# Attention score tiles as a ring of three single PSUM banks, exponentials of 512 columns, four banks for the max pass

## The chip, the cores and the metric

The kernel runs on one core of one Trainium2 chip. The metric is device time in microseconds of one launch, median of the runs shown. All durations below come from one profiled execution of the kernel before.

## The reference

One transformer layer on x of shape (2, 2048, 256), in float32:

```
x = x + attention(layernorm(x))          # 16 heads of 16, scores * decay_mask before the softmax
x = x + ffn(layernorm(x))                # W1, W2 quantized to -1, 0, 1; relu between, 1024 wide

scores = q k^T / sqrt(16) * decay_mask   # decay_mask[h, q, k] = sum_n mix[h, n] * decay[h, n] ** |q - k|
probs  = softmax(scores);  out = probs v;  out Wo^T + bo
```

## The kernel before

Three stages follow each other: a token block (layer norm, q, k, v), the attention, and the feed-forward network. The change lies in the attention, which fills most of the span.

**Steps and slots.** The attention works in 16 steps (2 sequences by 8 pairs of heads), each of 32 *slots*. `for_steps` writes all 16 steps out one after the other, and every engine runs its own list of instructions. The order is fixed by hand in `step` of each engine; nothing reorders it but the semaphores. Four *units* of eight slots make a step: 2 heads by 2 halves of the queries. The softmax needs the row maximum first, so a max pass runs 12 slots (`LEAD`) ahead of the exponentials.

**One slot on PE** (`step` under `@block.tensor`) issues in this order: max pass items 0 and 1, score tile 2s, item 2, score tile 2s+1, item 3, then the products of the slot before (`products(s - 1)`). In one slot of each unit a transpose of the maxima (`turn_max`, L1506) is added.

- *Max pass* (`max_scores`, L1492): an item fills one 512-column bank of `ring`. DVE reduces it (L1272, L1274, L1276) and gives the bank back by `ring_free`. `ring` has three such banks and a fourth, `acc`, in which the products accumulate.
- *Score tile* (`scores`, L1523 and L1520): 128 keys by 1024 queries in two adjoining banks. There are two tiles, `tile0` and `tile1`, so four banks. A tile comes in two kinds, by `score_parts`: *plain* (two matmuls of 512 columns) or *diagonal* (512 columns in one bank; 256, 128 and a float32 transpose of 128, the raw block, in the other). A slot has two tiles of one kind, and half of the slots are of each kind. PE waits (`exp_done`) before tile t until the exponential of tile t-2 is done.
- *Exponential* (ACT, L1232): one instruction for the 1024 columns of a tile, from PSUM to `probs`. It waits for `tile_full`, which the last matmul of the tile raises.
- *Products* (`products`, L1539): four float32 matmuls of 512 columns, each 32 columns of the array wide, on the `probs` of the slot before.

**Also on ACT**, after the exponentials of some slots: a cast of 1024 columns for the next pair (`builder.cast`, L196, in slots 0, 1, 3, 4, 6, 8, 9, 11, 13 and 15 of a step), once per unit the copy of `acc` (`take_unit`, L1223, in slots 0, 8, 16 and 24, after `acc_full` by the last product of the unit), and once per unit a small copy (`repeat_max`, L1212). In slots 0 and 8 the copy of `acc` is followed by a cast.

**PSUM** has eight banks, all used: four for the tiles, three for `ring`, one for `acc`. The feed-forward network reuses them: `up` the four of the tiles, `attn` and `turn` the first two of `ring`, `down` the two behind them.

```
            pe.wait_ge(exp_done, EXPS * o + t + 1)      # scores(t): ACT raised it by 2 at the start
            ...
            act.wait_ge(tile_full, EXPS * o + t + 1)
            nc.scalar.activation(probs[:, t % 4], tile[t % 2][:]..., ACT.Exp, ...).then_inc(exp_done, 1)
```

Of the kernel before, what the change touches and what calls it, by code (L numbers as in the profile page):

```python
# [22 lines left out]
F32 = mybir.dt.float32  # L23
# [5 lines left out]
P = 128  # L29
# [656 lines left out]
UNIT_SLOTS = BLOCKS // 2  # L686
UNITS = 4
LEAD = UNIT_SLOTS + 4
RING = 3
ITEMS = 4  # L690
RED_SLOT, TURN_SLOT = 4, 5
RING_STEP = ITEMS * SLOTS + UNITS
AHEAD_ITEMS = ITEMS * LEAD + 1
EXPS = 2 * SLOTS
W_TURNS = 8
TOTAL_BANK = RING - 1
INVERT_SLOTS = (9, 10)
ATTN_SLOT, TOTAL_SLOT, ROOT_SLOT, Z_SLOT, SPLIT_SLOT = 22, 23, 24, 25, 26
W_SLOT = SLOTS - 5
# [38 lines left out]
def attention_and_ffn_block(nc, a, keep, builder, scr, out):  # L738
# [7 lines left out]
    with ExitStack() as ctx:  # L746
# [20 lines left out]
        cut = sb("cut", [P, 2])  # L767
        neg_cut = sb("neg_cut", [P, 2])
        heads_out = sb("heads_out", [P, 2, 512])
        tile = [ctx.enter_context(nc.psum_tensor(f"tile{t}", [P, 2, 512], F32)) for t in range(2)]  # L770
        ring = ctx.enter_context(nc.psum_tensor("ring", [P, RING + 1, 512], F32))
        acc = ring[:, RING]

# [28 lines left out]

        def up(f):

            return tile[f // 2 % 2][:, f % 2]


        tile_full = sem("tile_full")
# [34 lines left out]

        def turn_bank(q):

            return ring[:, (TOTAL_BANK + q) % RING]

        sums_loaded = [sem(f"sums_loaded{u}") for u in range(2)]
        x_loaded = [sem(f"x_loaded2_{u}") for u in range(2)]
# [317 lines left out]
        @block.scalar  # L1167
        def _(act):
            def cast(c, builds):
                if c == 0:  # L1170
                    act.wait_ge(qk_in, builder.loaded(builds))
                    for h in range(2):
                        act.wait_ge(raw_in[h], 2 * PART_DMAS * QUADS * builds)
                level, side = builder.at(c)
                if side == 0 and level in (0, 2):
                    for h in range(2):
                        for done in (q_in[h][0][level // 2], q_in[h][1][level // 2], k_in[h][level // 2]):
                            act.wait_ge(done, PART_DMAS * QUADS * builds)
                builder.cast(act, c, builds)

            def root(g):
                act.wait_ge(sqrt_in, g + 1)
                nc.scalar.activation(rstd[:], rstd[:], ACT.Sqrt).then_inc(sqrt_out, 1)

            def split_z(g):
                act.wait_ge(turned, g + 1)
                nc.scalar.copy(z_hi[:], turn[:]).then_inc(z_hi_ready, 1)  # L1187

            def split_heads(g):
                u = g % 2  # L1190
                act.wait_ge(heads_ready, g + 1)
                nc.scalar.copy(heads_hi[u], heads[u]).then_inc(heads_hi_ready, 1)

            def relu(g, f):
                bias = keep["b1_col"][:, f:f + 1]
                act.wait_ge(up_done, FC * g + f + 1)
                nc.scalar.activation(h_hi[:, f], up(f), ACT.Relu, bias=bias)  # L1197
                nc.scalar.activation(hidden[:, f], up(f), ACT.Relu, bias=bias).then_inc(up_taken, 1)  # L1198

            act.sem_inc(acc_free, 1)  # L1200
            for h in range(2):
                act.sem_inc(out_stored[h], QUADS)
            act.wait_ge(unit_ready, 1)
            for h in range(2):
                rows = k_stack[h][STACK:STACK + MAXROWS, 0:RAW].rearrange("p l x -> p (l x)")
                nc.scalar.copy(rows, unit[STACK:STACK + MAXROWS].broadcast_to([MAXROWS, RAW * SEQ])
                               ).then_inc(const_ready, 1)

            def repeat_max(par, count):

                act.wait_ge(max_ready, count)
                nc.scalar.copy(max_repeated[:], row_max[:, par].unsqueeze(1).broadcast_to([P, MAXROWS * RAW, UNIT_SLOTS])  # L1212
                               ).then_inc(repeated_ready, 1)


            nc.scalar.activation(warm[:], ident[:, 0:1], ACT.Exp)
            repeat_max(0, 1)
            act.sem_inc(exp_done, 2)
            def step(i, o, more):
                def take_unit(u):  # L1220
                    act.wait_ge(acc_full, UNITS * i + u + 1)
                    act.wait_ge(out_stored[u % 2], QUADS * (2 * i + u // 2 + 1))
                    nc.scalar.copy(heads_out[:, u % 2], acc[:]).then_inc(acc_free, 1)  # L1223

                for s in range(SLOTS):
                    act.wait_ge(probs_used, SLOTS * o + s + 1)
                    for t in (2 * s, 2 * s + 1):
                        u = s // UNIT_SLOTS + 1
                        if s % UNIT_SLOTS == TURN_SLOT and t % 2 and (more or u < UNITS):
                            repeat_max(u % 2, UNITS * i + u + 1)  # L1230
                        act.wait_ge(tile_full, EXPS * o + t + 1)
                        nc.scalar.activation(probs[:, t % 4], tile[t % 2][:].rearrange("p a b -> p (a b)"), ACT.Exp,  # L1232
                                             scale=1.0 / (SCALE * SCALE * HEAD_DIM ** 0.5)).then_inc(exp_done, 1)
                    if s % UNIT_SLOTS == 0 and (s > 0 or o > 0):
                        take_unit(s // UNIT_SLOTS - 1)
                    for c in range(CHUNKS):
                        if more and hi_slot[c] == s:
                            cast(c, i + 1)
                    if not more and s == ROOT_SLOT:
                        root(0)  # L1240
                    if not more and s == SPLIT_SLOT:
                        split_z(0)
                if o == STEPS - 1:
                    take_unit(UNITS - 1)

            for_steps(step)
            for g in range(GROUPS):
                for f in range(FC):
                    relu(g, f)
                    if f == 3 and g + 1 < GROUPS:  # L1250
                        root(g + 1)
                    if f == 4 and g + 2 < GROUPS:
                        split_heads(g + 2)
                if g + 1 < GROUPS:
                    split_z(g + 1)

        @block.vector
        def _(dve):
# [41 lines left out]
            def invert(g):  # L1300
                u = g % 2
                dve.wait_ge(p_sums_loaded[u], 2 * QUADS * (g // 2 + 1))
                if g >= 2:
                    dve.wait_ge(inv_stored[u], QUADS * (g // 2))
                nc.vector.tensor_tensor(p_sums[:], p_sums_in[:, u, 0], p_sums_in[:, u, 1], ALU.add).then_inc(p_sums_added, 1)
                dve.wait_ge(p_sums_added, g + 1)
                nc.vector.reciprocal(inv[:, u], p_sums[:]).then_inc(inv_ready, 1)
# [164 lines left out]
        def _(pe):  # L1472
# [36 lines left out]
            def scores(t, o):  # L1509

                u, kb = t // BLOCKS, t % BLOCKS
                h, half = u // 2, u % 2
                pe.wait_ge(exp_done, EXPS * o + t + 1)
                started = set()
                for level, first, width in score_parts(kb, half):
                    col = first - half * HALF
                    bank, at = col // 512, col % 512
                    out = tile[t % 2][:, bank, at:at + width]
                    if level == RAW:
                        last = nc.tensor.matmul(out, diag[h][:, kb], ident[:], is_transpose=True,  # L1520
                                                start=bank not in started, stop=True, skip_group_check=True)
                    else:
                        last = nc.tensor.matmul(out, k_stack[h][:, level, kb * P:(kb + 1) * P],  # L1523
                                                q_stack[h][:, half, level, col:col + width],
                                                start=bank not in started, stop=True, skip_group_check=True)
                    started.add(bank)
                last.then_inc(tile_full, 1)

            def products(j, o):

# [2 lines left out]
                h = u // 2  # L1533
                for par in range(2):
                    t = 2 * j + par
                    pe.wait_ge(exp_done, EXPS * o + t + 3)
                    for qt in range(2):
                        row = (2 * par + qt) * ROWS
                        last = nc.tensor.matmul(acc[row:row + ROWS], v_ones[h][:, t % BLOCKS],  # L1539
                                                probs[:, t % 4, qt * 512:(qt + 1) * 512],  # L1540
# [29 lines left out]
            def up_product(g, f):  # L1570
                if f == 0:
                    pe.wait_ge(z_hi_ready, g + 1)
                if g == 0 and f == 0:
                    pe.wait_ge(w_taken, W_TURNS // 2)
                if FC * g + f >= 4:
                    pe.wait_ge(up_taken, FC * g + f - 3)
                for part in (z_hi, z_lo):
# [7 lines left out]
            def down_bias(g):  # L1585
                if g == 0:
                    pe.wait_ge(b2_ready, 1)
                    pe.wait_ge(w_taken, W_TURNS)
                    pe.wait_ge(acc_free, UNITS * STEPS + 1)
                else:  # L1590
                    pe.wait_ge(result_ready, g)
                for t in range(TILES):
# [17 lines left out]
            def turn_w(q):  # L1610
# [2 lines left out]
                pe.wait_ge(ternary_ready, m + 1)  # L1613
                if q == 1:
                    pe.wait_ge(z_lo_ready, 1)
                if q >= RING:
                    pe.wait_ge(w_taken, q - RING + 1)
                for j in range(4):
                    if m == 0:
                        src = rows[:, (q % 2) * 4 + j, (q // 2) * P:(q // 2 + 1) * P]  # L1620
# [121 lines left out]
```

## Time and profile before

| | |
|---|---|
| runs | 1788.88, 1789.5, 1789.95 us (median 1789.5) |
| profiled execution, first to last instruction | 1787.4 us |
| PE busy | 1744.3 us, 98% |
| DVE busy | 1558.8 us, 87% |
| ACT busy | 1345.2 us, 75% |
| POOL busy | 776.5 us, 43% |

The profiled execution is known by its span of 1787.4 us; the median of the runs is 2.1 us above it. PE is TensorE (matmuls), PEld its weight loads, DVE VectorE, ACT ScalarE, POOL GpSimd. The records of matmuls overlap, since a matmul is still draining while the next streams: a busy share of PE says that something was in flight, and the time from the start of one matmul to the start of the next says how fast they go through. The chain of waits gives the pieces by that second measure.

### The profile page before, as it was taken

To read this page: it belongs to the slowest core of one execution; us is meant where nothing else is said; L and a number is where in the kernel's file an instruction comes from. 1 tells how busy PE (TensorE), PEld (TensorE's weight loads), DVE (VectorE), ACT (ScalarE), POOL (GpSimd) and SP (SyncE) were. 2 spreads that over 40 slices of the span, in tenths; PEclk is the share of its full clock that TensorE was granted. 3 is DMA by queue.
4 is the path that set the end of the run, shared out by engine and by line. 5 is a ranking of instruction groups with operands and counts; after the bars stand their busy time and mean duration, and the time that the engine had idled before them with its cause. 6 is when DMAs were issued, how large, how long until landed. Compare 5 with 4: busy or idle time off the path is not lost.

```text
span 1787.4 us, 31962 instructions
## 1 busy us (share of the span) xinstructions
PE 1744.3 (98%) x11858; PEld 775.6 (43%) x11858; DVE 1558.8 (87%) x3664; ACT 1345.2 (75%) x1558; POOL 776.5 (43%) x405
## 2 busy tenths in 40 slices
PE   7979999999999999999999999999999999998998
PEld 4524444444444444444444444444444444444666
DVE  5879988999899989898999999898989999987885
ACT  5748687878787777878787878687878787667565
POOL 4009182726354554637271809181727364150110
PEclk9959999999999999999999999999999999999999
DMA  6884747474655546464637373747474645444541
GB/s 199 274 211 106 157 97 162 97 157 101 134 118 120 134 107 139 99 153 104 149 90 156 83 155 86 153 95 161 97 162 97 142 108 112 115 123 110 136 120 36
DMA packets 177835, 230.33 MB, mean 129 GB/s; under 512 B 92640, under 2 KB 113520, under 8 KB 167536
## 3 DMA queue, kind: packets, MB, share of 16 engines
q1 hardware_dynamic: 175744, 227.61, 54.6%
q8 instruction: 94, 1.54, 0.4%
q0 software_dynamic: 80, 0.54, 0.2%
q14 instruction: 61, 0.50, 0.1%
q10 hardware_dynamic: 1856, 0.14, 0.1%
HBM read 65.94 MB, written 36.45 MB: 57 GB/s over the span
## 4 chain that ended last, share of the span: by engine, by line
PE 87%; DVE 5%; ACT 1%; issue 1%; ACTq 0%; DVEq 0%
PE ring L1539 28%; PE ring L1492 27%; PE tile L1523 23%; PE tile L1520 3%; PE tile L1581 2%; PE ring L1600 2%; DVE part_max L1272 1%; PE ring L1506 1%; DVE qk L1362 1%; DVE z_lo L1358 1%; DVE stats L1334 1%; DVE decayed L1330 0%; ACT z_hi L1187 0%; PE ring L1567 0%; DVE lo L1314 0%
## 5 line engine op out<-in xcount | busy, mean ns | idle before, releaser
L1232 ACT ACTIVATE probs<-tile 128x1024 f32<-128x1024 f32 x1024 | 1000.3, 1023 | 331.4 <-PE tile L1520 183.8
L1272 DVE TENSOR_REDUCE part_max<-ring 128x1 f32<-128x512 f32 x1536 | 964.9, 683 | 122.1 <-PE ring L1492 120.1
L1492 PE MATMUL ring<-k_stack,q_stack 96*128 96x512 f16 (+2 forms) x3072 | 714.5, 314 | 11.2 <-SPq L211 9.7
L1523 PE MATMUL tile<-q_stack,k_stack 98*128 98x512 f16 (+2 forms) x2560 | 585.0, 326 | 0.3
L1539 PE MATMUL ring<-probs,v_ones 128*32 128x512 f32 x4096 | 546.8, 605 | 0.0
L1492 PEld LDWEIGHTS ring<-k_stack,q_stack 96*128 96x128 f16 x3072 | 263.9, 99 | 511.5 <-DVE part_max L1272 393.2
L1101 POOL TENSOR_TENSOR diag<-diag,row_max 128x1024 f32<-128x1024 f32 x64 | 121.6, 1900 | 629.9 <-DVE row_max L1285 629.9
L1523 PEld LDWEIGHTS tile<-q_stack,k_stack 98*128 98x128 f16 x2560 | 249.6, 98 | 275.0 <-ACT probs L1232 5.9
L188 POOL TENSOR_TENSOR decayed<-qk,table_in 128x1024 f32<-128x1024 f32 x120 | 282.9, 2363 | 8.0
L1274 DVE TENSOR_REDUCE part_max<-ring 128x1 f32<-128x384 f32 x512 | 279.6, 546 | 0.7 <-PE ring L1492 0.7
L202 POOL TENSOR_TENSOR lo<-decayed,hi 128x1024 f16<-128x1024 f32 x120 | 256.7, 2139 | 9.9 <-ACT hi L196 9.9
L1276 DVE CUSTOM_DVE_ANT_0 diag<-ring,mask 128x128 f32<-128x128 f32 x512 | 143.5, 280 | 2.0
L202 POOL TENSOR_TENSOR lo<-qk,hi 128x1024 f16<-128x1024 f32 x30 | 64.1, 2136 | 183.7 <-ACT hi L196 183.7
L1520 PE MATMUL tile<-ident,diag 128*128 128x128 f32 x512 | 143.1, 280 | 0.0
L196 ACT CAST hi<-decayed 128x1024 f16<-128x1024 f32 x128 | 133.8, 1045 | 6.8 <-POOL decayed L188 3.0
L1539 PEld LDWEIGHTS ring<-probs,v_ones 128*32 128x32 f32 x4096 | 81.0, 108 | 56.9 <-issue 3.0
L1520 PEld LDWEIGHTS tile<-ident,diag 128*128 128x128 f32 x512 | 71.6, 140 | 6.8
L1197 ACT ACTIVATE diag<-tile,b_col 128x512 f16<-128x512 f32 x64 | 44.0, 688 | 40.0 <-PE tile L1581 40.0
L1362 DVE TENSOR_TENSOR qk<-probs,diag 128x512 f16<-128x512 f32 x64 | 45.0, 703 | 27.7 <-ACT probs L1198 27.7
L1106 POOL TENSOR_TENSOR diag<-diag,bo_all 128x1024 f32<-128x1024 f32 x8 | 18.8, 2354 | 108.6 <-DMA diag<-in_x 108.6
L1198 ACT ACTIVATE probs<-tile,b_col 128x512 f32<-128x512 f32 x64 | 43.9, 686 | 0.0
L1600 PE MATMUL ring<-hi,diag 128*128 128x256 f16 x256 | 38.5, 273 | 5.1 <-DVE qk L1362 5.0
(154 smaller groups left out, 967.8 us busy)
## 6 DMA issues: line engine op xcount, KB each, us to landing
q_stack<-hi SPq DMA_DIRECT2D x320, 128.0 KB, 3.8
k_stack<-hi SPq DMA_DIRECT2D x128, 256.0 KB, 4.3
q_stack<-lo SPq DMA_DIRECT2D x160, 128.0 KB, 3.1
table_in<-table_scratch SPq DMA_DIRECT2D x64, 256.0 KB, 8.1
k_stack<-lo SPq DMA_DIRECT2D x64, 256.0 KB, 3.7
out_scratch<-heads_out SPq DMA_DIRECT2D x64, 256.0 KB, 3.3
k_stack<-hi SPq DMA_DIRECT2D x64, 128.0 KB, 3.4
lo<-out_scratch SPq DMA_DIRECT2D x32, 256.0 KB, 5.3
```

Of the source, the lines that this page charges most:

```text
L188: ops.tensor_tensor(self.source(c), self.half_view(self.qk[:], level, side), self.factors(level, side), ALU.mult).then_inc(self.decayed_re ...
L196: self.nc.scalar.copy(self.half_view(self.hi[:, level], level, side), self.source(c)).then_inc(self.hi_ready, 1)
L202: ops.tensor_tensor(self.half_view(self.lo[:, level], level, side), self.source(c), self.half_view(self.hi[:, level], level, side), ALU.su ...
L1101: nc.gpsimd.tensor_tensor(part, part, row_max[:, half].unsqueeze(2).broadcast_to([P, UNIT_SLOTS, P]), ALU.subtract).then_inc(diag_ready, 1)
L1232: nc.scalar.activation(probs[:, t % 4], tile[t % 2][:].rearrange("p a b -> p (a b)"), ACT.Exp, scale=1.0 / (SCALE * SCALE * HEAD_DIM ** 0. ...
L1272: nc.vector.tensor_reduce(out[:, k:k + 1], ring_bank(n), AX.X, ALU.max).then_inc(ring_free, 1)
L1274: nc.vector.tensor_reduce(out[:, 3:4], ring_bank(n)[:, 0:3 * P], AX.X, ALU.max).then_inc(blocks_seen, 1)
L1276: nc.vector.tensor_tensor_reduce(out=diag[h][:, q], in0=ring_bank(n)[:, 3 * P:4 * P], in1=mask[h][:], scale=1.0, scalar=-3.0e38, op0=ALU.m ...
L1492: last = nc.tensor.matmul(ring[:, n % RING, col:col + width], q_stack[h][0:STACK, q // UNIT_SLOTS, level, q0:q0 + P], k_stack[h][0:STACK, ...
L1520: last = nc.tensor.matmul(out, diag[h][:, kb], ident[:], is_transpose=True, start=bank not in started, stop=True, skip_group_check=True)
L1523: last = nc.tensor.matmul(out, k_stack[h][:, level, kb * P:(kb + 1) * P], q_stack[h][:, half, level, col:col + width], start=bank not in s ...
L1539: last = nc.tensor.matmul(acc[row:row + ROWS], v_ones[h][:, t % BLOCKS], probs[:, t % 4, qt * 512:(qt + 1) * 512], start=(j % UNIT_SLOTS = ...
```

## The change

The two double banks become one tensor `tile` of three single banks, and the bank that this frees goes to `ring`, now four banks for the max pass and `acc` behind them. A bank n = 4s .. 4s+3 of a slot holds half a tile. PE waits before bank n until the exponential of bank n-3 is done, and raises `tile_full` per bank. ACT issues four exponentials of 512 columns per slot in place of two of 1024, each on one bank. The products wait per bank. The order of the work on PE stays but for the diagonal tiles, whose parts are now issued bank by bank. The feed-forward network takes `acc` as its fourth `up` bank; a wait on DVE is added in `invert`; the turned weights keep their three banks.

```diff
-RING = 3
+RING = 4
+TILE_BANKS = 3
+W_BANKS = 3
...
-EXPS = 2 * SLOTS
+EXPS = 4 * SLOTS
...
-        tile = [ctx.enter_context(nc.psum_tensor(f"tile{t}", [P, 2, 512], F32)) for t in range(2)]
+        tile = ctx.enter_context(nc.psum_tensor("tile", [P, TILE_BANKS, 512], F32))
...
-            return tile[f // 2 % 2][:, f % 2]
+            return acc if f % 4 == TILE_BANKS else tile[:, f % 4]
...
-            act.sem_inc(exp_done, 2)
+            act.sem_inc(exp_done, TILE_BANKS)
...
-                    for t in (2 * s, 2 * s + 1):
+                    for n in range(4 * s, 4 * s + 4):
                         u = s // UNIT_SLOTS + 1
-                        if s % UNIT_SLOTS == TURN_SLOT and t % 2 and (more or u < UNITS):
+                        t, half = n // 2, n % 2
+                        if s % UNIT_SLOTS == TURN_SLOT and n % 4 == 2 and (more or u < UNITS):
                             repeat_max(u % 2, UNITS * i + u + 1)
-                        act.wait_ge(tile_full, EXPS * o + t + 1)
-                        nc.scalar.activation(probs[:, t % 4], tile[t % 2][:].rearrange("p a b -> p (a b)"), ACT.Exp,
+                        act.wait_ge(tile_full, EXPS * o + n + 1)
+                        nc.scalar.activation(probs[:, t % 4, half * 512:(half + 1) * 512],
+                                             tile[:, (EXPS * o + n) % TILE_BANKS], ACT.Exp,
...
@@ invert @@
+                if g >= 1:
+                    dve.wait_ge(inv_ready, g)
...
-                pe.wait_ge(exp_done, EXPS * o + t + 1)
-                started = set()
-                for level, first, width in score_parts(kb, half):
...
-                last.then_inc(tile_full, 1)
+                for x in range(2):
+                    n = EXPS * o + 2 * t + x
+                    pe.wait_ge(exp_done, n + 1)
+                    parts = [p for p in score_parts(kb, half) if (p[1] - half * HALF) // 512 == x]
...
+                        out = tile[:, n % TILE_BANKS, at:at + width]
...
+                    last.then_inc(tile_full, 1)
...
-                    pe.wait_ge(exp_done, EXPS * o + t + 3)
                     for qt in range(2):
+                        pe.wait_ge(exp_done, EXPS * o + 2 * t + qt + 1 + TILE_BANKS)
...
+                if g == 0 and f == TILE_BANKS:
+                    pe.wait_ge(acc_free, UNITS * STEPS + 1)
```

**Where instructions move.** On PE, one plain slot in the middle of a unit. `tile` is the score banks, `ring<-k_stack` the max pass, `ring<-probs` the products. Before:

```order
L1492 MATMUL ring<-k_stack,q_stack 128x512 [waits ring_free] x2
L1523 MATMUL tile<-q_stack,k_stack 128x512 [waits exp_done]
L1523 MATMUL tile<-q_stack,k_stack 128x512
L1492 MATMUL ring<-k_stack,q_stack 128x512 [waits ring_free]
L1523 MATMUL tile<-q_stack,k_stack 128x512 [waits exp_done]
L1523 MATMUL tile<-q_stack,k_stack 128x512
L1492 MATMUL ring<-k_stack,q_stack 128x256 [waits ring_free]
L1492 MATMUL ring<-k_stack,q_stack 128x128 x2
L1539 MATMUL ring<-probs,v_ones 32x512 [waits exp_done]
L1539 MATMUL ring<-probs,v_ones 32x512
```

and the same slot now:

```order
L1498 MATMUL ring<-k_stack,q_stack 128x512 [waits ring_free] x2
L1530 MATMUL tile<-q_stack,k_stack 128x512 [waits exp_done] x2
L1498 MATMUL ring<-k_stack,q_stack 128x512 [waits ring_free]
L1530 MATMUL tile<-q_stack,k_stack 128x512 [waits exp_done] x2
L1498 MATMUL ring<-k_stack,q_stack 128x256 [waits ring_free]
L1498 MATMUL ring<-k_stack,q_stack 128x128 x2
L1545 MATMUL ring<-probs,v_ones 32x512 [waits exp_done] x4
```

No matmul was added or taken away and none of these changed place; each 512-column score matmul and each product now has a wait of its own. On ACT, a slot with a cast behind it, before:

```order
L1232 ACTIVATE probs<-tile 128x1024 [waits tile_full,probs_used]
L1232 ACTIVATE probs<-tile 128x1024 [waits tile_full]
L196 CAST hi<-decayed 128x1024 [waits decayed_ready]
```

and now:

```order
L1235 ACTIVATE probs<-tile 128x512 [waits tile_full,probs_used]
L1235 ACTIVATE probs<-tile 128x512 [waits tile_full] x3
L196 CAST hi<-decayed 128x1024 [waits decayed_ready]
```

The cast stays behind the last exponential of its slot.

## Rows read from the trace of the kernel before

**Rows 1.** The page: an engine's busy time, and PE's granted clock in 40 slices.

```profile
PE 1744.3 (98%) x11858; PEld 775.6 (43%) x11858; DVE 1558.8 (87%) x3664; ACT 1345.2 (75%) x1558; POOL 776.5 (43%) x405
...
PEclk9959999999999999999999999999999999999999
```

**Rows 2.** Windows over one diagonal and one plain slot: length, busy time, clock, DMA.

```profile
702.50:705.47 2.97, 2.97 (x23) 1.37 (x22) 2.55 (x7) 2.18 (x3) 2.83 (x3) 1.00 1.04 221
705.47:708.31 2.84, 2.84 (x19) 1.05 (x18) 2.66 (x8) 2.84 (x4) 2.84 (x2) 1.00 0.08 24
```

**Rows 3.** Chain of waits, core stretch, two slots: start us, us, what.

```profile
701.96 0.54 PE ring L1492 x2
702.50 0.38 PE tile L1523 x3
702.88 0.12 PE tile L1520
...
703.93 1.00 PE ring L1539 x8
704.93 0.54 PE ring L1492 x2
705.47 0.43 PE tile L1523 x2
705.90 0.22 PE ring L1492
...
706.78 1.00 PE ring L1539 x8
```

**Rows 4.** Groups by line and form: busy us, mean ns | idle before, releaser.

```profile
L1232 ACT ACTIVATE probs<-tile 128x1024 f32<-128x1024 f32 x1024 | 1000.3, 1023 | 331.4 <-PE tile L1520 183.8 <-PE tile L1523 144.3
L1523 PE MATMUL tile<-q_stack,k_stack 98*128 98x512 f16 x1536 | 500.3, 380 | 0.3
...
L1198 ACT ACTIVATE probs<-tile,b_col 128x512 f32<-128x512 f32 x64 | 43.9, 686 | 0.0
...
L1223 ACT COPY heads_out<-ring 128x512 f32<-128x512 f32 x64 | 37.5, 586 | 1.2 <-PE ring L1539 1.2
...
L1187 ACT CAST z_hi<-ring 128x1024 f16<-128x1024 f32 x8 | 8.1, 1013 | 3.4 <-PE ring L1567 3.4
```

**Rows 5.** Timeline at 702 us, exponential after an idle ACT, products: start, us, what.

```profile
702.72 0.28 PE L1520 MATMUL tile<-ident,diag 128*128 128x128 f32 x1
...
703.09 1.94 ACT L1232 ACTIVATE probs<-tile 128x1024 f32<-128x1024 f32 x2 [0.85 <-PE tile L1520]
...
703.86 0.16 PEld L1539 LDWEIGHTS ring<-probs,v_ones 128*32 128x32 f32 x8
```

**Rows 6.** Chain of waits, last step, where PE waited for an exponential.

```profile
1595.62 1.95 ACT probs L1232 x2
1597.57 0.05 issue
1597.62 0.60 PE tile L1523 x2
```

**Rows 7.** Line 1492 at 704 us: ns min/median/max; the 390 is behind the products.

```profile
L1492 PE MATMUL ring<-k_stack,q_stack x3: 379/379/390, 704.9 to 705.7; 96*128 96x512 f16 x3
```

**Rows 8.** Timeline at 344 us: a new slot, and ACT with copy and cast.

```profile
344.60 0.11 PEld L1492 LDWEIGHTS ring<-k_stack,q_stack 96*128 96x128 f16 x2 [0.84 <-DVE part_max L1272]
...
344.76 0.59 ACT L1223 COPY heads_out<-ring 128x512 f32<-128x512 f32 x1
...
345.25 1.05 ACT L196 CAST hi<-decayed 128x1024 f16<-128x1024 f32 x1
...
346.19 1.03 ACT L1232 ACTIVATE probs<-tile 128x1024 f32<-128x1024 f32 x1
```

**Rows 9.** Windows: the max pass alone (98 to 128), and slots without it.

```profile
98.00:128.00 30.00, 26.74 (x68) 6.76 (x68) 27.93 (x71) 15.66 (x5) 1.89 (x1) 0.50 0.82 177
1598.00:1602.30 4.30, 4.30 (x33) 1.60 (x32) 2.05 (x3) 3.61 (x5) 4.16 (x3) 1.00 0.04 9
```

**Rows 10.** Waits over the whole span: total us, times, longest.

```profile
PEld ring L1492 <- DVE part_max L1272: 393.2, 502, 1.0
```

**Rows 11.** Timeline of the last step, a weight load behind products.

```profile
1599.15 0.11 PEld L1506 LDWEIGHTS ring<-ident,max_repeated 128*64 128x64 f32 x1 [0.84 <-issue]
```

More of the change, by code:

```diff
@@ L693 @@
 AHEAD_ITEMS = ITEMS * LEAD + 1
-EXPS = 2 * SLOTS
+EXPS = 4 * SLOTS
 W_TURNS = 8
-TOTAL_BANK = RING - 1
+TOTAL_BANK = W_BANKS - 1
 INVERT_SLOTS = (9, 10)
@@ L844, in turn_bank @@
         def turn_bank(q):
-            return ring[:, (TOTAL_BANK + q) % RING]
+            return ring[:, (TOTAL_BANK + q) % W_BANKS]
         sums_loaded = [sem(f"sums_loaded{u}") for u in range(2)]
@@ L1512, in scores @@
                 h, half = u // 2, u % 2
-                pe.wait_ge(exp_done, EXPS * o + t + 1)
-                started = set()
-                for level, first, width in score_parts(kb, half):
[L1516 to L1526, printed above, removed]
-                last.then_inc(tile_full, 1)
+                for x in range(2):
+                    n = EXPS * o + 2 * t + x
+                    pe.wait_ge(exp_done, n + 1)
+                    parts = [p for p in score_parts(kb, half) if (p[1] - half * HALF) // 512 == x]
+                    for j, (level, first, width) in enumerate(parts):
+                        at = first - half * HALF - x * 512
+                        out = tile[:, n % TILE_BANKS, at:at + width]
+                        if level == RAW:
+                            last = nc.tensor.matmul(out, diag[h][:, kb], ident[:], is_transpose=True,
+                                                    start=(j == 0), stop=True, skip_group_check=True)
+                        else:
+                            last = nc.tensor.matmul(out, k_stack[h][:, level, kb * P:(kb + 1) * P],
+                                                    q_stack[h][:, half, level, first - half * HALF:first - half * HALF + width],
+                                                    start=(j == 0), stop=True, skip_group_check=True)
+                    last.then_inc(tile_full, 1)
             def products(j, o):
@@ L1588, in down_bias @@
                     pe.wait_ge(w_taken, W_TURNS)
-                    pe.wait_ge(acc_free, UNITS * STEPS + 1)
                 else:
@@ L1615, in turn_w @@
                     pe.wait_ge(z_lo_ready, 1)
-                if q >= RING:
-                    pe.wait_ge(w_taken, q - RING + 1)
+                if q >= W_BANKS:
+                    pe.wait_ge(w_taken, q - W_BANKS + 1)
                 for j in range(4):
```

## The prediction

> **What bounds the kernel now.** I read the page first: PE is busy 98% of the span at the full granted clock but for the ends [rows 1]. A busy PE need not be PE at its peak, so the next view is the chain of waits in a stretch of the core. All of its pieces are PE's [rows 3], and the window over each slot agrees: PE busy 2.97 of 2.97 us in a diagonal slot and 2.84 of 2.84 in a plain one, at clock 1.00 [rows 2]. The same pieces come back in every slot. A score matmul of 512 columns takes 0.22 us from start to start, which is what it has to stream, a score tile 0.43 or 0.50, the products 1.00. PE waits for nobody here. DVE works 2.55 and 2.66 us of such a slot [rows 2], so it is some 0.3 us from the bound and follows PE. ACT waits 331 us in all for PE before its exponentials [rows 4]. The path is PE's list of instructions, 512 slots long.
>
> **What the change adds and removes.** On PE not one matmul is added, removed or made shorter. Since no slot holds a wait of PE's that could go, a gain has no place to come from; the question is what waits come in.
>
> *Fourth bank for the max pass.* It lets PE write an item while DVE is one more reduction behind. The wait table puts 393 us of PEld's idle time on these reductions [rows 10], which looks like the prize. But the wait ends when the products have streamed: the same 0.84 us of idle PEld stands before a weight load in the last step that follows products and whose releaser is "issue", not DVE [rows 11]. I cost the fourth bank at 0. Its cover is the 1.00 us of products, which hides the reductions. DVE can't gain on PE either, since the order on PE is fixed.
>
> *Bank ring of three, plain slot.* Before, tile t waited for the exponential of t-2, issued a whole slot earlier. Now bank n waits for that of bank n-3. For the last bank of a slot (n3) that is the exponential of the first (n0) **of the same slot**. Banks n0, n1 and n2 wait for exponentials of the slot before, which had the 1.00 us of products to finish.
> - Time that PE has between the starts of n0 and n3, from the chain: n0 and n1 0.43, item 2 0.22, n2 0.22, together 0.87 [rows 3], 0.86 less rounded.
> - Time that the loop needs: the matmul of n0, 0.38 from start to its modelled end [rows 4]; to the exponential, 0.10 more (the transpose that starts at 702.72 and takes 0.28 is followed by an exponential at 703.09) [rows 5]; the exponential, D; from its end to PE's next start, 0.05 [rows 6]; 0.01 for a matmul whose weights weren't loaded ahead (390 ns against 379) [rows 7].
> - D isn't in the trace for 512 columns. From PSUM, 1024 columns took 1013 ns as a cast and 512 columns 586 as a copy, so 512 columns are worth 427. The exponential of 1024 took 1023; less 427 that is **0.596** [rows 4], spaced 0.49 apart, since the long ones are spaced 0.92 (two in 1.94, one of them 1.02) [rows 5]. Lower bound 0.51, half of 1023 with no fixed part; upper bound 0.69, the relu of 512 columns that reads a bias [rows 4]. I take 0.596, next to the copy's 0.586, whose form is nearest.
> - Loop 0.38 + 0.10 + 0.596 + 0.05 + 0.01 = 1.14, less 0.86 = **0.28 us** of idle PE per plain slot.
>
> *Diagonal slot.* The bank with the raw block takes 0.38 + 0.12 - 0.22 = 0.28 [rows 3]. With the raw block in n0: its transpose starts 0.16 in and ends 0.28 later, so the loop is 0.16 + 0.28 + 0.10 + 0.596 + 0.05 + 0.01 = 1.20 against 0.28 + 0.22 + 0.22 + 0.28 = 1.00. With it in n1: 1.14 against 0.93. Both give **0.20 to 0.21**.
>
> Nothing hides these stalls: item 3, the products and the next slot are queued behind n3 on PE. Items 2 and n2 already stand between and are counted.
>
> *Where ACT comes late to n0.* After slots 0 and 8 of a step ACT copies `acc` and then casts. The copy can't start before the unit's last product is done: it starts 0.16 us into the next slot, the next exponential 1.59 in [rows 8]. In the kernel before that delay is absorbed, the next need being a slot away. Now n0's exponential would start at 0.44 + 0.48 = 0.92 (plain) or 0.98 (raw) into the slot, so n3 comes 0.6 later still. Two slots in each of 15 steps: 30 x 0.61 = **18 us**. A cast alone does no harm: the four exponentials begin at 0.92 and the last ends at some 2.98 of a 3.1 us slot; with 0.94 of cast behind it ACT is free at about 3.8, before 3.1 + 0.92. Nor does `repeat_max` (0.13).
>
> *ACT's sum.* Four spaced 0.49 make 1.97 us per slot instead of 1.84, +66 us in all, beside PE. With casts and copies (0.37 per slot) ACT has 2.34 of 3.1: not the bound.
>
> *The rest at nothing:* the waits of the products per bank (exponentials of the slot before, long done; today all eight of their weight loads pass in 0.16 us, across the wait that stands in their middle [rows 5]), the order within diagonal tiles (as many matmuls), `invert`, the fourth `up` bank (`acc` is free before the network begins). Longer slots give POOL and the loads more time; they were not waited for.
>
> **Sum.** In 500 slots with the max pass, 248 plain x 0.28 = 69 us and 252 diagonal x 0.202 = 51. Late copies 18. The last 12 slots have no items 2 between, but there PE already waits for exponentials [rows 6], so the loop of three banks adds only about 0.2 us to the slots that wait for nothing else, 2 us. Together **140 us**. Against the profiled span, 1787 + 140 = 1927; the median of the runs stood 2.1 above that span, so 1789.5 + 140 = **1929.5 us**.
>
> **Rivals.**
> 1. *D is long* (0.69, as the relu). The loop grows by 0.09: 500 x 0.09 = 45, and with some casts now late to n0, about 50 more: **1980 us**. For it: an exponential may fetch a bias as the relu does. Against: at 1024 columns it costs 10 ns more than a plain cast. 11%.
> 2. *D is short* (0.51): 500 x 0.085 = 43 less, **1887 us**. That there is a fixed part is seen in the copy (586, not 507) [rows 4]. 5%.
> 3. *PE's clock falls.* In the max pass alone, where PE waits for DVE between its matmuls, the granted clock is 0.50, 1.2 GHz; in slots of the last step where PE stood idle for exponentials it stayed at 1.00, 2.4 GHz [rows 9]. If the new idle in every slot let it fall in a tenth of the slots, each would cost another 2.84 less 0.28: 51 x 2.56 = 131 us, **2060 us**. 3%. The Trainium skill, TensorE: Matmul & The Clock Gate, section on a second failure mode (psum-queue depth-cycling), says that short idles of PE as it goes through PSUM banks make the clock alternate between its two levels; by that rule this rival is the rule and not the exception. The trace so far does not bear it out: the last step had longer idles at 1.00.
> 4. *The fourth bank pays* (the side below). If the wait table is right in that PE's weight loads are held by DVE, the loads may start one reduction earlier, 0.60 of the 0.84 us: 512 x 0.60 = 307 gained, 140 lost, **1622 us**. It decides from 0.27 us per slot on. For it: [rows 10]. Against: PE is streaming products in that time, and [rows 11]. 3%, and 1% that it just balances.
>
> **How the numbers follow.** The forecast has 77%: 1905 (late copies cost nothing and the tail too) to 1955 (D 0.62 and copies later). The range takes in rivals 1 and 2 at their ends, **1887 to 1980**, and leaves out 3 and 4 and what is beyond. A measurement of this kernel can tell about 0.2% from no change. Faster by more: 0.03; within: 0.01; slower: 0.96.
>
> **What would show it.** In the profile after: a group of ACT exponentials 128x512 x2048 of about 596 ns; a wait of PEld's score load for the exponential in nearly every slot, some 0.2 to 0.5 us of idle load each; slots of 3.11 to 3.12 (plain) and 3.17 (diagonal), 3.7 behind the copy with cast, at clock 1.00; the chain alternating between PE and ACT; DVE's wait for `ring` up by as much as PE's stall; no change in the wait of the max items. The prediction is wrong if slots stay at 2.84, if D is outside 0.51 to 0.69, if the last bank of a slot isn't the one that waits, or if ACT has no idle time left.

## The result and the profile after

The changed kernel takes **1928.85 us** (median of 4 runs, 1928.51 to 1930.11) against 1789.72 (4 runs, 1788.88 to 1789.96): a ratio of 1.0784, 95% interval 1.077 to 1.0797, so 139 us slower. The profiled execution spans 1926.7 us, 139.3 more than before.

The page of the changed kernel, engines and PE's granted clock, where [rows 1] stood before:

```profile
span 1926.7 us, 32986 instructions
...
PE 1828.8 (95%) x11858; PEld 753.1 (39%) x11858; DVE 1581.8 (82%) x3664; ACT 1414.8 (73%) x2582; POOL 777.8 (40%) x405
...
PEclk9969999999999999999999999999999999999999
```

PE went from 98% to 95%. The granted clock stayed at full, 1.00 over the whole stretch from 135 to 1750 us. A page hardly shows a loss of 7.8%: 139 us of span came, of which 84.5 count as busy PE, because the records of matmuls cover most of each short wait. The groups by line, where [rows 4] stood:

```profile
L1235 ACT ACTIVATE probs<-tile 128x512 f32<-128x512 f32 x2048 | 1065.2, 602 | 387.3 <-PE tile L1530 284.4 <-PE tile L1527 94.4
...
L1530 PE MATMUL tile<-q_stack,k_stack 98*128 98x512 f16 x1536 | 545.0, 382 | 54.4 <-ACT probs L1235 28.8
...
L1530 PEld LDWEIGHTS tile<-q_stack,k_stack 98*128 98x128 f16 x2560 | 239.9, 98 | 473.6 <-ACT probs L1235 276.5 <-issue 0.8
```

and the last of these before:

```profile
L1523 PEld LDWEIGHTS tile<-q_stack,k_stack 98*128 98x128 f16 x2560 | 249.6, 98 | 275.0 <-ACT probs L1232 5.9 <-issue 1.5
```

The exponential of 512 columns took 602 ns (0.596 forecast). The score matmul is as long as before (382 against 380 ns), so no work got slower. What is new is idle time before PE's score weight loads, 473.6 us in place of 275.0, and the exponentials as its releaser. The waits of the whole span:

```profile
PEld ring L1498 <- DVE part_max L1280: 320.0, 385, 0.8
ACT probs L1235 <- PE tile L1530: 284.4, 292, 3.0
PEld tile L1530 <- ACT probs L1235: 276.5, 515, 3.9
...
DVE part_max L1276 <- PE ring L1498: 198.0, 374, 0.6
...
PEld ring L1498 <- DVE part_max L1276: 65.8, 96, 0.8
```

The third row is the stall: before, this wait came 9 times in the whole program and held 5.9 us; now it comes 515 times in 512 slots and holds 276.5 us of idle PEld. Loads stood idle for 275.0 us before too, with PE busy 98% of the span, so this is more than PE lost: about half of it, 139 us, is time added. The first and last row together are the wait that the fourth bank was to relieve: 385.8 us in 481 times, where [rows 10] had 393.2 in 502. It is still there, with another reduction's name on it. DVE's own wait for PE (the fourth row; `L1276` is the reduction that was `L1272`) went from 120.1 to 198.0 us: DVE was slowed by PE, not PE by DVE.

The chain of waits over one plain slot, start us, us, what, where [rows 3] stood:

```profile
809.62 0.54 PE ring L1498 x2
810.15 0.23 PE tile L1530
810.39 0.02 issue
810.41 0.02 ACTq L1234
810.42 0.04 issue
810.47 0.61 ACT probs L1235
811.08 0.05 issue
811.12 0.39 PE tile L1530
811.51 0.22 PE ring L1498 x3
811.74 0.99 PE ring L1545 x8
```

From 809.62 to 812.73 the slot takes 3.11 us (2.84 before). The path leaves PE behind n0 (the 0.23) and runs through 0.08 of issue and queue, 0.61 of exponential, 0.05 of issue, and back to n3 (the 0.39). Bank n1, item 2 and n2 don't appear: they are done inside that loop. What follows n3 has its old lengths. In a diagonal slot the stall shows less, since the long bank gives PE more to do:

```profile
803.26 0.54 PE ring L1498 x2
803.80 0.38 PE tile L1530 x3
804.18 0.12 PE tile L1527
804.30 0.22 PE ring L1498
804.52 0.22 PE tile L1530
804.74 0.03 issue
804.76 0.34 PE tile L1530 x2
805.10 0.12 PE tile L1527
805.22 0.22 PE ring L1498 x3
805.44 0.99 PE ring L1545 x8
806.44 0.54 PE ring L1498 x2
```

3.18 us from 803.26 to 806.44, against 2.97. Here the view keeps to PE and shows the loop only as 0.03 of issue ahead of n3. The rest is in the next row: 0.34 for the first two matmuls of n3, which took 0.17 where they followed others at once (as the same pair does in [rows 3], 0.38 less the 0.22 of the long one). The view counts n2 to its modelled end, and n3, started afresh behind it, is counted from start to modelled end too, which is 0.17 longer. 0.03 + 0.17 = 0.20. A gap on PE has to be measured from slot to slot, not read off an "issue" row.

The slot behind a copy and a cast, on the timeline (start, us, engine):

```profile
540.73 2.07 ACT L1235 ACTIVATE probs<-tile 128x512 f32<-128x512 f32 x4 [1.18 <-PE tile L1527]
...
543.08 0.59 ACT L1225 COPY heads_out<-ring 128x512 f32<-128x512 f32 x1 [0.29 <-PE ring L1545]
...
543.57 1.05 ACT L196 CAST hi<-qk 128x1024 f16<-128x1024 f32 x1
...
544.51 2.06 ACT L1235 ACTIVATE probs<-tile 128x512 f32<-128x512 f32 x4
...
545.16 0.10 PEld L1530 LDWEIGHTS tile<-q_stack,k_stack 98*128 98x128 f16 x1 [0.82 <-ACT probs L1235]
```

The copy starts when the last product of the unit is done, the cast follows, n0's exponential begins 1.58 us into the slot, which starts at 542.93 (0.15 before the copy, as in [rows 8]), and n3 waits for it to 545.17. This slot takes 3.785 us. The trace has 29 such slots, all of this length.

### The profile page after: what moved, and what is told of

Same layout as the page of the kernel before. It is cut to its first block, busy times and chain, and to the rows that moved or that the text cites. A ratio compares the mean times of both kernels' runs of the same rounds, so it can differ in the third digit from the quotient of the medians.

```text
span 1926.7 us, 32986 instructions
## 1 busy us (share of the span) xinstructions
PE 1828.8 (95%) x11858; PEld 753.1 (39%) x11858; DVE 1581.8 (82%) x3664; ACT 1414.8 (73%) x2582; POOL 777.8 (40%) x405
## 4 chain that ended last, share of the span: by engine, by line
PE 76%; ACT 11%; issue 4%; DVE 4%; ACTq 0%; DVEq 0%
PE ring L1545 27%; PE ring L1498 21%; PE tile L1530 20%; ACT probs L1235 9%; PE tile L1527 3%; PE ring L1607 2%; PE tile L1589 1%; DVE part_max L1276 1%; PE ring L1512 1%; DVE qk L1368 1%; ACT heads_out L1225 1%; DVE z_lo L1364 0%; PE ring L1589 0%; DVE stats L1340 0%; PE ring L1573 0%
## 5 line engine op out<-in xcount | busy, mean ns | idle before, releaser
L1235 ACT ACTIVATE probs<-tile 128x512 f32<-128x512 f32 x2048 | 1065.2, 602 | 387.3 <-PE tile L1530 284.4
L1276 DVE TENSOR_REDUCE part_max<-ring 128x1 f32<-128x512 f32 x1536 | 965.7, 684 | 202.9 <-PE ring L1498 198.0
L1530 PE MATMUL tile<-q_stack,k_stack 98*128 98x512 f16 (+2 forms) x2560 | 687.7, 328 | 59.8 <-ACT probs L1235 30.2
L1530 PEld LDWEIGHTS tile<-q_stack,k_stack 98*128 98x128 f16 x2560 | 239.9, 98 | 473.6 <-ACT probs L1235 276.5
L1278 DVE TENSOR_REDUCE part_max<-ring 128x1 f32<-128x384 f32 x512 | 283.5, 554 | 18.3 <-PE ring L1498 18.2
L1199 ACT ACTIVATE diag<-tile,b_col 128x512 f16<-128x512 f32 x48 | 33.1, 689 | 33.3 <-PE tile L1589 33.3
L1225 ACT COPY heads_out<-ring 128x512 f32<-128x512 f32 x64 | 37.5, 586 | 19.0 <-PE ring L1545 19.0
```

What stands on the lines that cost most here:

```text
L1235: nc.scalar.activation(probs[:, t % 4, half * 512:(half + 1) * 512], tile[:, (EXPS * o + n) % TILE_BANKS], ACT.Exp, scale=1.0 / (SCALE * S ...
L1276: nc.vector.tensor_reduce(out[:, k:k + 1], ring_bank(n), AX.X, ALU.max).then_inc(ring_free, 1)
L1278: nc.vector.tensor_reduce(out[:, 3:4], ring_bank(n)[:, 0:3 * P], AX.X, ALU.max).then_inc(blocks_seen, 1)
```

## Experiments

Slots below are from the starts of the products' matmuls in each trace, medians over the steps, given as plain / diagonal. The kernel before: 2.841 / 2.971; the changed one: 3.113 / 3.178.

### The score ring back to four banks

```diff
-RING = 4
-TILE_BANKS = 3
+RING = 3
+TILE_BANKS = 4
```

(and the wait for `acc_free` back in `down_bias`)

> Score ring of four single banks, max pass back on three, exponentials still 512 wide: only the depth of the score ring is undone. Theory (the stall is the wait of bank n3 for the exponential of n0 in the same slot): bank n now waits for that of n-4, a whole slot back, so PE's slots return to 2.84 and 2.97 us and the time to 1790 us (1788 to 1793), although ACT has 66 us more of exponentials than before. Rival (narrower exponentials are the cost, ACT has become the bound): the time stays near 1929, at least 1855 (1790 + 66).

Measured: 1788.88 us against 1788.16 for the kernel before on the same chip, ratio 1.0003 (0.9993 to 1.0012); slots 2.841 / 2.974. Exponentials of this kernel and a piece of its chain:

```profile
L1235 ACT ACTIVATE probs<-tile 128x512 f32<-128x512 f32 x2048 | 1064.0, 606 | 257.9 <-PE tile L1530 184.5 <-PE tile L1527 72.4
```

```profile
904.15 0.54 PE ring L1498 x2
904.69 0.43 PE tile L1530 x2
905.12 0.22 PE ring L1498
905.34 0.43 PE tile L1530 x2
905.77 0.22 PE ring L1498 x3
906.00 0.99 PE ring L1545 x8
```

The halved exponentials cost 64 us of ACT and nothing of the time. All of the 139 us come from the depth of the ring; the rival, ACT as the bound, is out.

### The max pass back to three banks, the rest as changed

```diff
+MAX_BANKS = 3
...
-                    if n + AHEAD_ITEMS - RING + 1 > 0:
-                        pe.wait_ge(ring_free, RING_STEP * o + n + AHEAD_ITEMS - RING + 1)
+                    if n + AHEAD_ITEMS - MAX_BANKS + 1 > 0:
+                        pe.wait_ge(ring_free, RING_STEP * o + n + AHEAD_ITEMS - MAX_BANKS + 1)
...
-                        last = nc.tensor.matmul(ring[:, n % RING, col:col + width],
+                        last = nc.tensor.matmul(ring[:, n % MAX_BANKS, col:col + width],
```

(and the same in `turn_max` and in DVE's `ring_bank`)

> The change with its max pass on three banks, the fourth left idle: only the gift to the max pass is taken back. Theory (the fourth bank is worth nothing, PE's idle weight loads before the max items are the products streaming): 1929 us, within 2 us. Rival (the fourth bank pays part of the loss back): slower than 1929 by what it pays, up to 307 us if 0.60 us per slot, 47 us if only the 0.09 us between the two spacings behind a group of products (545 against 453 ns).

Measured: 1928.99 us, ratio to before 1.0783 (1.0767 to 1.0799); slots 3.113 / 3.178. The fourth bank brought nothing that can be measured.

### Item 3 ahead of bank n3

```diff
-                    scores(2 * s + 1, o)
+                    scores(2 * s + 1, o, (0,))
+                    late = s % BLOCKS == BLOCKS - 1
+                    if late:
+                        scores(2 * s + 1, o, (1,))
+                    if ahead:
+                        max_scores(s, s + LEAD, (3,), i, o)
+                    if not late:
+                        scores(2 * s + 1, o, (1,))
...
-                    if ahead:
-                        max_scores(s, s + LEAD, (3,), i, o)
```

In slots 15 and 31 the old order has to stay, since item 3 releases the stack that n3 still reads.

> The change with item 3 of the max pass issued before score bank n3 in place of behind it, in 30 of 32 slots. Theory: 0.22 us more work lies between n0 and n3, so the plain slots' stall of 0.28 shrinks to about 0.06 and the diagonal one's 0.21 to 0: slots of 2.89 to 2.91 and 2.97, 1827 us (1820 to 1835). Rival (PE waits for something that doesn't depend on what stands between n0 and n3, such as the extra waits themselves): 1929.

Measured: 1828.6 us in one run (before 1789.34); slots 2.890 / 2.975, 3.177 in slots 15 and 31, which kept the old order, and 3.56 behind copy and cast. 100 us are won back by moving item 3 past one bank. PE had as many waits as before, so it is not the waits that cost but what stands inside the loop.

### No cast behind the copy

```diff
-        hi_slot = (0, 1, 3, 4, 6, 8, 9, 11, 13, 15)
+        hi_slot = (1, 2, 3, 4, 6, 7, 9, 11, 13, 15)
```

> The change with no cast behind the copy of acc: the casts of slots 0 and 8 go elsewhere (slots 1, 2, 3, 4, 6, 7, 9, 11, 13, 15). Theory: 30 slots lose 0.6 to 0.67 us each, 19 us, so 1910 us, and no slot of 3.78 is left. Rival (those slots are long because the copy alone is late, or because POOL's chain behind the casts is late): under 5 us change, or slower.

Measured: **1966.25 us**, slower than the change by 37 us (ratio to before 1.0989, 1.0972 to 1.1005). The theory held for the slots behind the copies, which fell to 3.18 and 3.11. The total went the way of the rival, a slower kernel through POOL's chain: slot 4 grew to 5.5 us or more in all 15 steps that have casts, and slot 5 to 4.2 to 4.6 in 12 of them. ACT's timeline at one slot 4:

```profile
771.82 1.10 ACT L1235 ACTIVATE probs<-tile 128x512 f32<-128x512 f32 x2
773.02 4.65 POOL L188 TENSOR_TENSOR decayed<-qk,table_in 128x1024 f32<-128x1024 f32 x2
775.47 1.04 ACT L196 CAST hi<-decayed 128x1024 f16<-128x1024 f32 x1 [2.55 <-POOL decayed L188]
776.42 2.05 ACT L1235 ACTIVATE probs<-tile 128x512 f32<-128x512 f32 x4
777.06 0.10 PEld L1530 LDWEIGHTS tile<-q_stack,k_stack 98*128 98x128 f16 x1 [2.98 <-ACT probs L1235]
```

The third cast waits 2.55 us for a product of POOL. POOL makes that product only behind the rest of the second cast, and I had moved the second cast one slot later and left the third where it was. All exponentials queue behind the waiting cast, and PE's n3 behind them (2.98 us of idle PEld, 2.48 of idle PE).

That explains slot 4 and not slot 5. The windows (length, busy time, clock, DMA) of slots 4 and 5 of this step, and of slot 5 of another step:

```profile
772.11:777.61 5.50, 3.02 (x21) 1.00 (x19) 2.76 (x7) 2.95 (x6) 5.36 (x3) 1.00 0.21 55
777.61:782.10 4.49, 4.49 (x21) 1.20 (x19) 2.72 (x7) 2.99 (x7) 4.49 (x4) 0.62 0.01 4
...
568.22:571.34 3.12, 3.02 (x21) 0.97 (x19) 2.56 (x7) 2.99 (x7) 3.12 (x3) 1.00 0.00 0
```

In the long slot 5 PE is busy all the time, and its granted clock is lower. Within it, from 777.80 to 781.20 us, it is 0.50 (1.2 GHz). In each of the 15 steps PE stood idle for 2.48 us in slot 4. In 12 of them the clock fell to 0.50 behind that; in three it stayed at 1.00 and slot 5 took 3.11 (there slot 8 took 3.5). The page has a 9 in each of its clock slices there and does not show this.

I went on from the cause in slot 4 and shifted the first casts together:

```diff
-        hi_slot = (0, 1, 3, 4, 6, 8, 9, 11, 13, 15)
+        hi_slot = (1, 2, 4, 5, 7, 9, 10, 12, 14, 15)
```

> The change with the casts in slots 1, 2, 4, 5, 7, 9, 10, 12, 14 and 15: no cast behind the copy of acc, and the distances between the first casts as in the kernel before, so that POOL's products are there when ACT comes to them. In the run with the casts of slots 0 and 8 moved, slots 1 and 9 fell to 3.18 and 3.11 as the theory has it, but slots 4 and 5 grew to 5.5 and 4.4, with a cast that waited 2.55 us for POOL. Theory: 30 slots lose 0.6 to 0.67 us and none gains, 1910 us (1907 to 1914). Rival (moving casts always starts POOL's chain late): still above 1929.

Measured: 1910.28 us (ratio to before 1.0685, 1.0667 to 1.0703), no slot of 3.78 left. The late copies cost 18.6 us, as one run less the other gives (1928.85 - 1910.28; the kernel before took 1789.7 and 1788.8 us beside them, so this is good to about 1 us). Against this run, the core of the one with the unlucky casts is 56.3 us longer: 36.8 in slot 4 and 15.8 in slot 5. The wait in slot 4 is 15 x (5.50 - 3.18) = 35 us of that; some 18 us, by estimate, are what the lower clock cost, namely what is left of these two slots.

### A longer exponential

```diff
-                                             tile[:, (EXPS * o + n) % TILE_BANKS], ACT.Exp,
+                                             tile[:, (EXPS * o + n) % TILE_BANKS], ACT.Exp, bias=no_bias[:],
```

> The change with exponentials that read a bias of zeros from a tile of its own, a way to make D longer. Theory: each ns of D is a ns of every one of 500 slots, 0.5 us per ns. If D goes from 602 to the relu's 687 ns, 1973 us (slots of 3.20 and 3.27); if the bias costs nothing, D and the time stay. Rival (the wait isn't the loop through ACT's latency): time unchanged with D longer.

Measured: 1979.76 us in one run; slots 3.203 / 3.267, and more in the slots behind a cast.

```profile
L1236 ACT ACTIVATE probs<-tile,no_bias 128x512 f32<-128x512 f32 x2048 | 1249.7, 693 | 282.4 <-PE tile L1532 212.3 <-PE tile L1529 69.6
```

(`no_bias` is a tile of one column of zeros.) D rose by 91 ns (693 against 602) and the slots by 90 and 89. That gives 45 us over 500 slots; the other 6 of the 51 are slots in which ACT, now with less slack, came to n0 late (3.26 behind casts). An exponential with a bias from a tile behaves as the relu did.

### A ring of two banks

```diff
+SCORE_BANKS = 2
...
-            act.sem_inc(exp_done, TILE_BANKS)
+            act.sem_inc(exp_done, SCORE_BANKS)
```

(and `% SCORE_BANKS` for the banks of scores and exponentials, `+ SCORE_BANKS` in the products' wait)

> The change with a score ring of two banks, one step further. Theory: n2 waits for n0's exponential and n3 for n1's, of the same slot. Loop 1.15 against 0.65 between them: 0.50 us more per slot, slots of 3.61 and 3.67, 2180 us (2160 to 2200), clock still 1.00 in the core. Rival (the clock rule: many short idles of PE make the granted clock alternate): the granted clock under 1.00 in part of the core, and over 2250 us.

Measured: 2177.93 us in one run; slots 3.600 / 3.667. The granted clock in 40 slices, and the window over the core (the 1.00 is the clock):

```profile
PEclk9879999999999999999999999999999999999999
```

```profile
135.00:1990.00 1855.00, 1642.07 (x10118) 576.03 (x10118) 1377.26 (x3199) 1273.12 (x2286) 740.60 (x354) 1.00 0.44 98
```

With some 0.76 us of idle array in each plain slot, 21% of it, the clock stayed at full (2.4 GHz) through the core. That bears on the rule cited as a rival, from the Trainium skill, TensorE: Matmul & The Clock Gate, on psum-queue depth-cycling: this kernel cycles through PSUM banks with a short idle of PE in every slot, and with those idles no alternation is seen in the core of this run or of the changed kernel. The clock did go back and forth in the core of the run with the casts moved, and in the one below that has this placing too, each time behind an idle of PE of 2.4 to 2.7 us, which is not one of the short ones of the ring.

### Score banks and max items alternating

```diff
-                        max_scores(s, s + LEAD, (0, 1), i, o)
+                        max_scores(s, s + LEAD, (0,), i, o)
...
-                    scores(2 * s, o)
+                    scores(2 * s, o, (0,))
+                    if ahead:
+                        max_scores(s, s + LEAD, (1,), i, o)
+                    scores(2 * s, o, (1,))
                     if ahead:
                         max_scores(s, s + LEAD, (2,), i, o)
-                    scores(2 * s + 1, o)
+                    scores(2 * s + 1, o, (0,))
...
```

(item 3 and n3 as in the run above, swapped in slots 15 and 31)

> The change with max items and score banks alternating on PE and nothing moved on ACT. Theory: no stall but in the 30 slots behind copy and cast, which keep some 0.6 to 0.7 us: slots 2.85 and 2.98 (as in the run with both edits, in all slots but 4 and 5), 1812 us (1806 to 1818). Rival (the 1870 us of the run with both edits came from the alternation): near 1870.

Measured: 1814.45 us (ratio 1.0147, 1.0132 to 1.0162); slots 2.850 / 2.978, with 3.56 left behind copy and cast. The order alone gives back 114 of the 139 us.

With both edits, first with the unlucky placing of the casts:

> The change with max items and score banks alternating (item 0, n0, item 1, n1, item 2, n2, item 3, n3; the last two swapped in slots 15 and 31) and no cast behind the copy of acc (casts in slots 1, 2, 3, 4, 6, 7, 9, 11, 13, 15). Theory: 1.3 us lie between n0 and n3 against a loop of 1.15, so no stall is left and three banks do what four did: slots 2.84 and 2.97, 1792 us (1789 to 1797). The fourth bank of the max pass brings nothing below that. Rival (waits per bank keep weight loads from being pulled ahead, or the alternation costs): above 1805.

Measured: 1869.97 us (ratio 1.0452, 1.0434 to 1.047). Missed, and for what was found above: slot 4 took 5.5 to 5.9 us in all 15 steps through a cast that waited for POOL, and behind it the granted clock fell to 0.50 in 11 of them (slot 5 at 4.5 to 5.4, slot 6 at up to 4.7). In the other four slot 8 took 4.3, its cast waiting 1.4 us for POOL. The other slots were at 2.85 / 2.98. Then with the casts shifted together:

> Both: alternating order on PE and the casts in slots 1, 2, 4, 5, 7, 9, 10, 12, 14 and 15. Theory: no stall of the score ring is left; 1794 us (1790 to 1798), some 0.01 us per slot above the kernel before, as in the slots of the run with both edits (2.85 and 2.98 against 2.84 and 2.97). It doesn't beat the kernel before, since PE's stream of matmuls is the same and the fourth bank of the max pass hides nothing that wasn't hidden. Rival (with DVE fed more evenly and a fourth bank, DVE's slack turns into a gain): under 1786.

Measured: **1802.92 us** (ratio 1.0081, 1.0066 to 1.0096), 9 us over what I expected. The slots are right but for two in each step: slot 16 takes 3.34 and slot 11 3.05. The timeline at slot 16:

```profile
838.74 1.04 ACT L196 CAST hi<-decayed 128x1024 f16<-128x1024 f32 x1 [0.63 <-POOL decayed L188]
...
839.69 2.05 ACT L1235 ACTIVATE probs<-tile 128x512 f32<-128x512 f32 x4
...
840.34 0.10 PEld L1530 LDWEIGHTS tile<-q_stack,k_stack 98*128 98x128 f16 x1 [0.36 <-ACT probs L1235]
```

The last cast, moved next to the one before it, waits 0.63 us for POOL; the cast ahead of slot 11 waits 0.17. These two slots are 0.36 + 0.20 us a step, 8.4 us in 15 steps. I did not try a further placing, as even without them (1794.5) the kernel would not beat the one before.

## Why the prediction was right

It said 1929.5 us, and 1928.85 was measured. The mechanism is the one that was forecast, and the terms hold one by one to within 4 us. That the sum came out within 1 us is luck: the plain slots were put 4 us too high, and the other three terms together about 3 us too low.

- **PE's list is the path and no slot has slack.** Right. Where the stall is taken away (four banks), the slots return to their old lengths to within 0.003 us, with 64 us more work on ACT.
- **D = 0.596 us**: 0.602. The longer exponential showed the slope: 90 ns of slot for 91 ns of D.
- **Plain slot +0.28, diagonal +0.20 to 0.21**: 3.113 - 2.841 = 0.272 and 3.178 - 2.971 = 0.207. The 31 plain slots that hold the transpose of the maxima lose only 0.20 (3.24 against 3.04), for a cause that I did not look for. So the plain slots cost 217 x 0.272 + 31 x 0.20 = 65 us, where I had 69, and the diagonal ones 252 x 0.207 = 52, where I had 51. The chain shows the loop in its parts: 0.08 where I took 0.10, 0.61 with the part to the exponential's end, 0.05 back.
- **Copy and cast, 18 us**: 18.6, by taking them away. There were 29 such slots, not 30 (slot 0 of the first step has no copy behind it). The added length is 3.785 less 3.113 or 3.178, 0.64 on average, against 0.61: I took the diagonal slot's value for all, and half of them are plain, at 0.67.
- **Fourth bank 0**: 0 within the intervals, in a run of its own. The row by which I judged it (the same idle time before a weight load that no reduction holds [rows 11]) was the right one; the wait table's releaser was not.
- **The last 12 slots, 2 us**: in the trace of the changed kernel this stretch is 2.8 us longer than before. The run with four banks has it 2.6 us shorter, so it varies by as much as the term, and the term is not settled.
- Rival 1 is what the run with the bias became: 1979.8 for 1980. Rival 3 did not happen, even with almost three times the idle time per slot. But the ground on which I set it aside was misread: in the window of the last step in [rows 9] PE is busy 4.30 of 4.30 us, so it shows no idle of PE at the full clock. The trace before has such a window later, at 1609 to 1614 us: PE busy 1.82 of 5.00 us at 1.00. And the mechanism is real here: behind the longer idles of the moved casts the clock fell to 0.50. Which idles are too long, these runs do not show. Rival 4 is out by the run with three banks. Rival 2 never applied: ACT's fixed part per instruction is there.

Two of the signs were off. I looked for a chain alternating between PE and ACT: it does so in plain slots, but in diagonal ones it stays on PE. And DVE's wait was to grow by as much as PE's stall, but its row grew by 78 us of the 139. "A cast alone does no harm" holds only for a cast whose input is there, which the moved casts taught me, and only with this D: with the longer exponential the slots behind a cast took 3.26 in place of 3.20.

## What to carry to other kernels

Count a ring's depth in the consumer's round trip: find the producer's work that stands between bank n and the reuse of its place, and compare it with the matmul's end, the consumer's instruction and both hand-overs. Cutting tiles in half and keeping three of four halves shortens the distance from a whole slot to 0.86 us, while the round trip, with its fixed parts, falls only to 1.14; where it doesn't fit, moving other work into the loop gave back 100 and 114 of the 139 us. And a further bank is worth nothing where the producer was not waiting for a bank: the max pass gained nothing by its fourth.

When an instruction with a wait is moved in an in-order queue, its own inputs have to be followed: what stands behind it waits too.

When slots get longer next to a stall, read the granted clock of each slot and not only the page's row: a slot in which an engine waits for nobody can be long by its clock.

## What the runs showed that I had not expected

- The two placings of the casts differ by 56 us (1966.25 against 1910.28): 2.55 us of waiting for POOL on ACT became slots of 5.5 us on PE, and in 12 of 15 steps the granted clock fell to 0.50 behind PE's idle of 2.5 us, which made the next slot 4.4. By estimate 35 us are the wait and some 18 the clock.
- The page's busy share hid most of the loss: 84.5 us of the 139 count as busy PE.
- An exponential that names a bias tile took 693 ns against 602 without, on the same 512 columns. The relu with a bias and the copy without one lay 100 ns apart before [rows 4].
